# One-hot matrices of a graph network kernel built in four pieces with the destination as a scalar of each partition

## What is computed

```python
for l in range(3):                                         # three graph layers
    m = relu(x[src] + edge_attr @ We[l] + be[l])
    h = x + segment_sum(m, dst, num_segments=n)            # sums over the edges of a node
    x = layer_norm(relu(relu(h @ W1[l] + b1[l]) @ W2[l] + b2[l]))
...                                                        # relational attention
smax = segment_max(scores, dst, num_segments=N)            # typed attention, first pass: maxima
w = exp(scores - smax[dst]) / (segment_sum(...)[dst] + 1e-10)
agg = segment_sum(V[src] * w, dst, num_segments=N)         # second pass
...
h = relu(concat(x[src], x[dst], edge_attr) @ W1.T + b1)    # message pass
agg = segment_sum(h @ W2.T + b2, dst, num_segments=N)
```

## Time and profile before

| | us |
|---|---|
| median of 3 runs | 4971.89 (4968.58 to 4981.04) |
| the profiled execution | 4978.06, of it the profile's span 4976.0 |
| PE busy | 3122.3 (63%) |
| DVE busy | 2700.0 (54%) |
| POOL busy | 2927.5 (59%) |
| ACT busy | 721.8 (15%) |
| chain that ended last: POOL, issue, PE, DMA, DVE | 50%, 20%, 14%, 8%, 5% |

### The profile page before, as it was taken

The page is one execution under the profiler, slowest core; times in us unless marked ns, Lnnn a source line. Parts: engine busy times, 40 slices in busy tenths (PEclk is TensorE's granted clock), DMA queues, the critical chain, the costliest instruction groups (busy, mean ns, idle before and its releaser), DMA issues.

```text
span 4976.0 us, 85301 instructions
## 1 busy us (share of the span) xinstructions
PE 3122.3 (63%) x20716; PEld 2741.5 (55%) x20717; DVE 2700.0 (54%) x8043; ACT 721.8 (15%) x1742; POOL 2927.5 (59%) x2911
## 2 busy tenths in 40 slices
PE   0000098886777767776664557767777788667776
PEld 0000088885666656666454346545555688566665
DVE  5100088885444444444667955546666566655553
ACT  1000022222111111111110034420000000411111
POOL 3767677774777747777057877037777000067772
PEclk9999999997555555555765589875555699888886
DMA  6333255554222232223276279476656444033332
GB/s 218 75 89 77 74 154 148 156 153 88 79 76 76 74 61 76 76 75 76 71 208 175 85 199 227 118 206 173 171 171 170 96 126 126 5 91 92 91 92 45
DMA packets 643811, 577.27 MB, mean 116 GB/s; under 512 B 235163, under 2 KB 535800, under 8 KB 643576
## 3 DMA queue, kind: packets, MB, share of 16 engines
q0 software_dynamic: 99328, 211.51, 18.2%
q1 hardware_dynamic: 389624, 235.01, 16.3%
q10 hardware_dynamic: 154752, 129.55, 9.4%
HBM read 424.35 MB, written 151.40 MB: 116 GB/s over the span
## 4 chain that ended last, share of the span: by engine, by line
POOL 50%; issue 20%; PE 14%; DMA 8%; DVE 5%; ACT 1%; SPq 1%; DVEq 0%; POOLq 0%; ACTq 0%
POOL ring L811 29%; POOL HA L829 8%; POOL arena L838 8%; POOL slot_records L797 5%; PE ps L2282 3%; PE ps L2131 2%; DMA ring<-table_gine,idx 2%; DMA arena<-in_edge_attr 2%; DMA table_rel<-arena 1%; PE ps L2283 1%; PE ps L2149 1%; PE ps L2245 1%; DMA slot_records<-arena,slotr 1%; PE ps L1950 1%; DVE HA L854 1%
## 5 line engine op out<-in xcount | busy, mean ns | idle before, releaser
L811 POOL DMA_INDIRECT ring<-table_gine,idx x1248 | 1249.6, 1001 | 498.3 <-issue 370.2
L811 POOL DMA_INDIRECT ring<-table_msg,idx x416 | 398.3, 958 | 630.3 <-DMA table_msg<-arena 503.7
L854 DVE TENSOR_TENSOR mraw<-ps,ring 128x512 f32<-128x512 f32 x416 | 287.7, 691 | 779.4 <-DMA ring<-table_gine,idx 344.1
L838 POOL DMA_INDIRECT arena<-table_keys_values,idx x416 | 435.2, 1046 | 335.8 <-DVEq L186 207.3
L1993 PE MATMUL ps<-oh,msg 128*128 128x128 f32 x1664 | 423.4, 435 | 317.6 <-DVE HA L854 222.8
L829 POOL DMA_INDIRECT HA<-table_rel,idx x416 | 447.1, 1075 | 292.0 <-DMA table_rel<-arena 165.4
L1993 PEld LDWEIGHTS ps<-oh,msg 128*128 128x128 f32 x1664 | 364.5, 323 | 376.2 <-DVE HA L854 345.2
L854 DVE TENSOR_TENSOR HA<-HA,ps 128x128 f32 (+1 forms) x1664 | 476.3, 286 | 165.7 <-DVE HA L854 146.3
L1960 PE MATMUL ps<-wt,ear 65*128 65x128 f32 x2496 | 518.4, 378 | 16.0 <-DMA ear<-edge_attr_T 15.8
L797 POOL DMA_INDIRECT slot_records<-arena,slotr x400 | 392.8, 982 | 213.7 <-issue 123.2
L1960 PEld LDWEIGHTS ps<-wt,ear 65*128 65x128 f32 x2496 | 491.5, 292 | 16.9 <-issue 16.3
(11 more groups left out here) (379 smaller groups left out, 5911.3 us busy)
## 6 DMA issues: line engine op xcount, KB each, us to landing
ear<-edge_attr_T SPq DMA_DIRECT2D x312, 128.0 KB
ear<-slot_rows ACTq DMA_DIRECT2D x312, 128.0 KB
oh<-slot_rows ACTq DMA_DIRECT2D x104, 256.0 KB
slot_values<-HA SPq DMA_DIRECT2D x104, 256.0 KB
ring<-slot_values ACTq DMA_DIRECT2D x104, 256.0 KB
slot_values<-arena SPq DMA_DIRECT2D x104, 256.0 KB
ring<-slot_values SPq DMA_DIRECT2D x104, 256.0 KB, 3.0
slot_records<-msg SPq DMA_DIRECT2D x32, 650.0 KB, 11.6
```

The lines of the kernel that those rows point to most:

```text
L811: pool.indirect_dma_start(out=ring[:, k % 4, j, 0:width], out_offset=None, in_=table[:, :], in_offset=bass.IndirectOffsetOnAxis(ap=idx[:, ...
L838: pool.indirect_dma_start(out=kvring[:, k % 4, j, :], out_offset=None, in_=tab2[:, :], in_offset=bass.IndirectOffsetOnAxis(ap=idx5[:, k * ...
L854: return V.tensor_tensor(o, x, y, op)
```

## The change

In the graph layers, and in the first typed pass, the one-hots of a batch are made by four `tensor_scalar` of 128 x 128 in the place of one `tensor_tensor` of 128 x 512. The first operand is `iota_n` itself, and the destination is a scalar of each partition, one column of `dl` (`dl_end`). The semaphore is raised by the last of the four. The four few words for the change name the message pass as well; but `made is qg["onehot"]` holds for the graph layers alone, and the message pass calls with `qp["onehot"]`.

```diff
@@ onehot(made, used, buf, t, count)
                 if made is qg["onehot"] and t.of == 0:
                     dve.wait_ge(qs["fields"], t.n * 4 + 4)
+                if made is qg["onehot"]:
+                    for j in range(B):
+                        ins = V.tensor_scalar(buf[:, t.s4 % depth, j, :], iota_n[:, :], dl[:, bass.ds(t.k * B + j, 1)], None, ALU.is_equal)
+                    ins.then_inc(made, 1)
+                    return
                 tt(buf[:, t.s4 % depth], iota_n[:, :].unsqueeze(1).to_broadcast([P, B, P]),
                    dl[:, bass.ds(t.k * B, B)].unsqueeze(2).to_broadcast([P, B, P]), ALU.is_equal).then_inc(made, 1)
@@ end_onehots(t)
                 if t.late(4):
                     dve.wait_ge(qm["sums"], t.n - 3)
-                tt(oh[:, t.s4], iota_n[:, :].unsqueeze(1).to_broadcast([P, B, P]),
-                   dl_end[:, bass.ds(t.k * B, B)].unsqueeze(2).to_broadcast([P, B, P]), ALU.is_equal).then_inc(qm["onehot"], 1)
+                for j in range(B):
+                    ins = V.tensor_scalar(oh[:, t.s4, j, :], iota_n[:, :], dl_end[:, bass.ds(t.k * B + j, 1)], None, ALU.is_equal)
+                ins.then_inc(qm["onehot"], 1)
```

## The result

The changed kernel takes 4920.2 us in the median of ten runs (4910.0 to 4952.4), against 4971.3 (4959.5 to 4997.6) for ten runs of the kernel before beside it: a ratio of 0.990, 95% interval 0.987 to 0.993. That is 51 us less where 87 were forecast, 35 us above the forecast's value and inside its range. The profiled execution has a span of 4914.8 us against 4976.0, 61 us less. I read the stages in it first, as before the change.

The account below looks back on a forecast made before the run. POOL's gather issue was taken to bound four stages. Stretches removed, 96 us, less 8 for the pieces' own and 1 for queueing gave -87 us from 4978.1, so 4891, and 4885 us as median; range 4862 to 5050.

Parts of the forecast that it names:

- What bounds the kernel, and what stretches a gather: Four stages: POOL issues a gather every 1.25 us at best; a DVE one-hot delays it, ending 0.82 us after.
- Case A: Stages at POOL's pace: pieces let the gather in; 4885 us, own range 4860 to 4925, chance 0.45.
- B: Rival, layers and typed pass: the row of pieces holds the port as one; 4970 us, chance 0.20.
- C: Rival, layers and typed pass: the row takes the port ahead of the gather every batch; 5107 us, chance 0.28.
- D: Rival, layer 1: DVE becomes its bound, with pieces over 0.28 us apart; 4900 us, chance 0.07.
- Layers 2 and 3, 22 us each: Graph layers 2 and 3: all stretch of the gathers goes, 22 us in each.
- Layer 1, 11 us: Layer 1: a little under half of its 26 us stretch goes, as the permutation also runs each batch.
- The pieces' own stretches, 8 us: All changed stages: gathers stretched by the new pieces cost 8 us, bounds nothing and 83 us.
- DVE's time, +79 us: 416 batches: four pieces add 0.19 us of DVE work each, 79 us in all, lying beside the gathers.
- The typed pass, 41 us: First typed pass: 41 of its 42 us of stretched gathers go with the one-hot in pieces.
- What bounds next: The changed stages: still POOL, at 1.25 us a gather.
- its own weak point: Typed pass: forecast is wrong if a wait for its other loads takes the freed time; no size given.

Follow-up runs that it names:

- layers_only: The change in the three graph layers alone, the typed pass keeping its whole one-hot, against the kernel before: 4922.7 us, ratio 0.989.
- the rows ahead: The changed kernel with the typed pass's reset rows loaded one batch further ahead: 4909.3 us, ratio 0.986 against the kernel before.
- the two further edits: Layer 1's permutation and the typed pass's turned one-hot in four pieces; run on the changed kernel with reset rows loaded earlier: 6115.0 us, ratio 1.0042 against the kernel before.

## Why the prediction was right, and where its sum was not

- *What bounds the kernel, and what stretches a gather.* Right. Four stages went at POOL's pace, and the gathers of layers 2 and 3 came down to 945 ns. The rule of the earlier trace rows, 0.82 us from the moment at which DVE lets go, holds in the changed kernel too; it dates the entry of the gather of 1257.76 to the end of the first piece. What the prediction didn't see is that the form helps by itself: to hold a gather an operation must start 0.04 us ahead of it with two inputs, and 0.1 us with one source.
- *Case A against B and C.* Right for the layers. B asked for stretched gathers that end 0.82 us after the fourth piece, C for one gather in four at 1.6 to 1.7 us; neither is there. In the typed pass B is there in part: 12 gathers are held by the fourth piece, for 2.7 us. The time of the whole alone would not have told the cases apart, since the range of 4862 to 5050 holds A, B, D and a part of C; the stages do.
- *Layers 2 and 3, 22 us each.* Right: 23 each. *Layer 1, 11 us*: 9. What it left there was the permutation, as said: with that in pieces the stage gave 8 to 13 us more.
- *The pieces' own stretches, 8 us.* Too high for the layers, where they are none. *DVE's time, +79 us*: it is 100 us. A piece takes 305 ns in the layers against the 280 of the earlier trace rows, since it, and not the gather, waits when both begin together. That cost nothing, by the cover that was named.
- *The typed pass, 41 us.* This is the term that was mis-sized; it gave 15. I took nearly all of its stretch for the one-hot's, though in the earlier trace rows the gather of 3389.78 ends 0.81 us after L1420. I read that row only as a warning about operations in a row. It said also that L1420 holds a gather, and a one-hot in pieces leaves L1420 where it is: of the 17.4 us of stretch that are left 13.8 hang on it, and in the run with it in pieces too 10.8 are left in all. The stretch fell from 42.1 us to 17.4, 25 in place of 41. Even the 42.1 is one trace's: with the same code in the pass layers_only had 33.5.
- *What bounds next.* The forecast named its own weak point, that the freed time is taken by a wait for the pass's other loads, but put no term on it. It was 10 us: POOL's waits in the pass, 128.5 us with its issue, rose to 138.6. With the rows ahead they are 130.5. 24.7 - 10.1 = 14.6 is the gain of the trace.
- *The rest of the gap.* The profiled execution was 87 - 61 = 26 us short. The typed pass is 26 of it, "between" 11 and layer 1 2; against that stand 2 more in layers 2 and 3, 2 in the message pass, and the 8 and 1 us that were set aside for the pieces and for what is queued behind them. The 11 us between lie within what the other traces vary by.

The Trainium skill, page SBUF — State Buffer, section "SBUF: two separate sides", says that a one-source operation which uses both ports keeps POOL from writing descriptors, and so spoke against the change. The one-source operation of 512 columns shows it at 1258.91, where the gather is held to the operation's end; that the pieces use both ports no run shows. That the one who starts first has the ports for the whole instruction, as the section says, holds here only from a lead on: at 1274.24 the operation had begun 0.07 us ahead and the gather went through. A two-input operation, which by that section stands only against a POOL operation that reads SBUF, held the gathers more than the one-source form did, 21.6 against 2.4 us in layer 2 at the same 512 columns.

## What to carry to other kernels

Where a gatherer's queue sets the pace, look for gathers longer than the shortest and for what ends a fixed time before them; then make that operation short, and read one tensor instead of two if it can be had. Count the whole row of operations around it: the next one can hold the gather too. And take the gain only down to the next loop, here one of landings, loads and buffers that already stood in DVE's 112 us of waits for the rows; where loads landed late, the pieces and the two further edits together gained nothing (ratio 1.004).

## What I had not expected of the hardware

- An operation with two inputs and one with one source meet a gather differently at the same moment. Starting 0.07 to 0.08 us ahead of it, the first holds it to its end (1.43 us at 1371.63), the second doesn't (0.94 at 1274.24); starting 0.12 or 0.24 us ahead the second holds it as well (1.17 at 1294.22, 1.06 at 1259.15). The border is sharp in both, at 0.04 and at 0.09 to 0.10 us.
- Whether a row of pieces lets the gather in depends on something that these runs don't show: a gather that began 0.13 us into the row took 0.97 us in layer 2, one that began 0.08 us into it took 1.58 in the typed pass, to the end of the fourth piece; in the layers none that began so early was held at all. One difference is that another one-source operation follows in the typed pass; whether it is that is open.
- The same kernel took 4972.9 us (median of 7 runs) and later 6084.5 (17 runs) on the same chip, with adds that started 13.6 us later behind their gathers and nothing in the kernel changed. The packets of the gathers' queue took no more time in all, 18.2% of 16 engines over 4976.0 us in the trace of before and 14.0% over 6095.8 us, so the delay isn't in the time of the packets. Why it came is open.
